# A graph network kernel: beside the last 56 edge rows, cosines are blended in PSUM and weighed from there, ScalarE weighs the gathered rows, and one PSUM bank takes the step sums

## The reference, cut to what matters

```python
def hetsann_conv(feat, src, dst, etype, edge_weight, W, Al, Ar, ...):
    h = typed_linear(feat[src], W, etype)
    ...
    agg = jax.ops.segment_sum(h3 * att * edge_weight, dst)     # cut
x = _layernorm(x + L0(x))          # two such layers, heads 8 and 1
# L1: cosine of the two ends of an edge weighs the sum over its neighbours
Wh = x @ W + b
sim = sum(Wh[row] * Wh[col]) / (|Wh[row]| * |Wh[col]|)
base = adj_v * softplus(deg_coeff[0] * deg_v + deg_coeff[1]) * (row != col)
prop_pos = segment_sum((base * relu(sim))[:, None] * Wh[col], row)
prop_neg = segment_sum((base * -relu(-sim))[:, None] * Wh[col], row)
x = _layernorm(x + scale * (c0 * prop_pos + c1 * prop_neg + c2 * Wh))
```

## Time and profile before

| | |
|---|---|
| median of 3 runs | 4801.52 us (4799.81 to 4803.82) |
| the profiled execution | 4794.28 us, its span 4792.6 us |
| the last 56 rows, first gather to last addition | 3336.5 to 4466.7 us |
| the other units, until the last product | to 4719.3 us |
| what follows: result turned back, last normalisation, store | to 4792.6 us |

### The profile page before, as it was taken

One profiled execution on the slowest core, in us unless ns is written; L12 is line 12 of the kernel. 1 busy time (PEld: TensorE's weight loads), 2 busy tenths in 40 slices (PEclk: granted clock), 3 DMA queues, 4 the chain that ended last, 5 costly groups with the idle time before them and its releaser, 6 DMA issues. The chain is left out here.

```text
span 4792.6 us, 63834 instructions
## 1 busy us (share of the span) xinstructions
PE 3187.0 (66%) x16141; PEld 1906.6 (40%) x16141; DVE 3208.5 (67%) x5876; ACT 1384.8 (29%) x2465; POOL 3339.1 (70%) x3216
## 2 busy tenths in 40 slices
PE   2667777777777777775555555554678767487795
PEld 2344445445545544543343444443323232222222
DVE  4676776767776677775555555554588777487686
ACT  2422232323232323233322122222233222132352
POOL 0277777777777777773577777775777777777573
PEclk6798888988888898887777777776688879688897
DMA  1233332323332333232222222223356545255583
GB/s 52 98 94 93 94 98 85 102 85 100 92 99 89 96 94 96 90 98 85 91 80 71 65 78 71 71 71 102 89 157 172 149 120 153 75 166 155 159 245 108
DMA packets 355069, 502.09 MB, mean 105 GB/s; under 512 B 92892, under 2 KB 214749, under 8 KB 354574
## 3 DMA queue, kind: packets, MB, share of 16 engines
q1 hardware_dynamic: 251453, 394.51, 25.4%
q0 software_dynamic: 100352, 102.96, 10.1%
q10 hardware_dynamic: 2896, 0.59, 0.1%
HBM read 290.63 MB, written 207.16 MB: 104 GB/s over the span
## 5 line engine op out<-in xcount | busy, mean ns | idle before, releaser
L809 POOL DMA_INDIRECT frows<-messages,fidx x2352 | 2277.5, 968 | 848.5 <-issue 669.3
L889 PE MATMUL fps_b<-hot_key,hot_lo 128*128 128x343 f32 x3136 | 1233.8, 502 | 407.1 <-PEq L70 403.3
L948 DVE TENSOR_TENSOR strip<-strip,fps_b 128x343 f32 x1568 | 787.0, 502 | 541.7 <-DVEq L70 516.5
L1091 POOL DMA_INDIRECT lrows<-messages,lidx x784 | 879.2, 1121 | 271.2 <-issue 223.7
L879 PE MATMUL fps_sum<-hot,frows 128*64 128x80 f32 x4704 | 551.1, 301 | 601.9 <-PEq L70 601.9
L824 ACT ACTIVATE turned<-fps_t 128x512 f32<-128x512 f32 (+1 forms) x754 | 431.6, 572 | 1741.2 <-ACTq L70 1738.8
L889 PEld LDWEIGHTS fps_b<-hot_key,hot_lo 128*128 128x128 f32 x3136 | 541.6, 206 | 728.8 <-issue 679.1
L879 PEld LDWEIGHTS fps_sum<-hot,frows 128*64 128x64 f32 x4704 | 521.9, 194 | 693.0 <-issue 693.0
L918 DVE TENSOR_SCALAR hot_key<-iota_f,edge 128x343 f32<-128x343 f32 x1574 | 750.9, 477 | 0.1
L1236 ACT ACTIVATE pos<-l_c,coeff 128x896 f32<-128x896 f32 x392 | 394.6, 1007 | 725.2 <-PE l_c L1140 725.2
L1140 PE MATMUL l_c<-unit_t,unit_g 64*128 64x448 f32 x1568 | 460.9, 667 | 148.5 <-DVE acc L1278 89.1
(11 more groups left out here) (186 smaller groups left out, 1741.7 us busy)
## 6 DMA issues: line engine op xcount, KB each, us to landing
adj<-turned SPq DMA_DIRECT2D x696, 256.0 KB
edge<-adj SPq DMA_DIRECT2D x294, 448.0 KB
adj_x<-adj SPq DMA_DIRECT2D x98, 448.0 KB
frows<-messages,fidx POOLq DMA_INDIRECT x2352, 2.4
messages<-msg SPq DMA_DIRECT2D x14, 1120.0 KB, 4.6
lrows<-messages,lidx POOLq DMA_INDIRECT x784
adj<-turned SPq DMA_DIRECT2D x58, 64.0 KB
wh_g<-wh_rows SPq DMA_DIRECT2D x56, 32.0 KB, 1.7
```

The lines of the kernel that those rows point to most:

```text
L809: pool.indirect_dma_start(rows[:, q, k, :], None, tab_l[l].ap(), bass.IndirectOffsetOnAxis(ap=idx[:, q, k:k + 1], axis=0)).then_inc(s_got[ ...
L889: pe.matmul(ps_b[n % KB][:, 0:NT * TWIN], hot_lo[:, s % 2, k, :], hot_key[:, n % KB, :], start=True, stop=True).then_inc(s_b, 1)
L948: dve.tensor_tensor(part, part, ps_b[n % KB][:, 0:NT * TWIN].rearrange("p (h w) -> p h w", w=TWIN), ALU.add).then_inc(v, 1)
L1091: pool.indirect_dma_start(rows[:, q, k, :], None, tab_l[1].ap(), bass.IndirectOffsetOnAxis(ap=idx[:, q, k:k + 1], axis=0)).then_inc(s_got[ ...
```

## The change

It touches `last_rows` alone. The order is planned with five units a row in place of six (`OWN`), and eight calls of `some` stand ahead of row 0. While rows run (units 0 to 255, `in_place`; before, 271 units were planned beside the rows), the blend is written back to the PSUM buffer of the cosines, and the weighing that follows it at once on VectorE reads that PSUM buffer, multiplies by `adj` and writes `con`. The cosines of unit u + 2, which need the PSUM buffer, then wait for the weighing of u, not for its blend. The comparisons of a row are one VectorE instruction that reads the node numbers from a PSUM bank (`l_iota`) and no longer multiplies by the weight. ScalarE multiplies the 14 gathered pieces by the weight in four parts, each behind the positive part of a unit; TensorE's sum waits for the last part (`s_wm`). The indices of row r + 4 are written when row r has landed. `l_iota` takes a bank, and the step sums have one bank, `l_o`, in place of two: the first product of each visit waits for the `kept` of the visit before.

```diff
-            OWN = 6
+            OWN = 5
+            PARTS = ((0, 4), (4, 8), (8, 11), (11, 14))
...
             plan.append(("hot", 0))
+            some(8, 0)
             for r in range(n_rows):
                 if r + 1 < n_rows:
                     plan.append(("hot", r + 1))
-                some(OWN - 1, r)
+                for j in range(len(PARTS)):
+                    some(1, r)
+                    plan.append(("wt", r, j))
                 plan.append(("sum", r))
-                some(1, r)
+                some(OWN - len(PARTS), r)
                 plan.append(("add", r))
...
-                ps_o = [psum(f"l_o{k}", [P, 512], s4) for k in range(2)]
+                ps_o = psum("l_o", [P, 512], s4)
+                ps_iota = psum("l_iota", [P, 512], s4)
...
+                def in_place(u):
+                    return u < alone
+
                 def weigh(eng, u):
                     eng.wait_ge(s_blend, u + 1)
                     eng.wait_ge(s_adj[u % NA], 16 * (u // NA + 1))
-                    eng.tensor_tensor(con[u % CB], con[u % CB], adj_b[u % NA], ALU.mult).then_inc(s_con[count[u][0]], 1)
+                    if in_place(u) and u >= CB:
+                        eng.wait_ge(s_prod, u - CB + 1)
+                    eng.tensor_tensor(con[u % CB], ps_c[u % 2][:, :, 0:SB] if in_place(u) else con[u % CB], adj_b[u % NA], ALU.mult).then_inc(s_con[count[u][0]], 1)
...
                         if u >= 2:
-                            pe.wait_ge(s_blend, u - 1)
+                            if in_place(u - 2):
+                                weighed(pe, u - 2)
+                            else:
+                                pe.wait_ge(s_blend, u - 1)
...
-                        if u == lo and k >= 2:
-                            pe.wait_ge(s_o_free, k - 1)
+                        if u == lo and k >= 1:
+                            pe.wait_ge(s_o_free, k)
...
-                        pe.wait_ge(s_got[r % RB], (r // RB + 1) * JT * 16).then_inc(s_idx_free[r % RB], 1)
+                        pe.wait_ge(s_wm, r + 1)
...
+                        elif event[0] == "wt":
+                            r, j = event[1:]
+                            if j == 0:
+                                act.wait_ge(s_got[r % RB], (r // RB + 1) * JT * 16)
+                                if r + RB < n_rows:
+                                    indices(r + RB)
+                            for k in range(*PARTS[j]):
+                                at = (first_row + r) * JT + k
+                                last = act.activation(rows[:, r % RB, k, :], rows[:, r % RB, k, :], ACT.Copy, scale=edge[:, A_W, at:at + 1])
+                            if j == len(PARTS) - 1:
+                                last.then_inc(s_wm, 1)
...
-                        if u >= CB:
+                        if not in_place(u):
                             dve.wait_ge(s_prod, u - CB + 1)
-                        dve.scalar_tensor_tensor(con[u % CB], ps_c[u % 2][:, :, 0:SB], coeff[:, 5:6], pos[:, u % 2, :, :], ALU.mult, ALU.add).then_inc(s_blend, 1)
+                        dve.scalar_tensor_tensor(ps_c[u % 2][:, :, 0:SB] if in_place(u) else con[u % CB], ps_c[u % 2][:, :, 0:SB], coeff[:, 5:6], pos[:, u % 2, :, :], ALU.mult, ALU.add).then_inc(s_blend, 1)
...
-                        for j in range(JT):
-                            at = (first_row + r) * JT + j
-                            last = dve.tensor_scalar(hot[:, r % 2, j, :], iota_f[:, 0:WIN], edge[:, A_REL, at:at + 1], edge[:, A_W, at:at + 1], ALU.is_equal, ALU.mult)
-                        last.then_inc(s_hot, 1)
+                        at = (first_row + r) * JT
+                        dve.tensor_tensor(hot[:, r % 2, :, :], ps_iota[:, 0:WIN].rearrange("p (o c) -> p o c", o=1).to_broadcast([P, JT, WIN]),
+                                          edge[:, A_REL, at:at + JT].rearrange("p (k o) -> p k o", o=1).to_broadcast([P, JT, WIN]), ALU.is_equal).then_inc(s_hot, 1)
...
                             if u < len(units):
                                 blend(u)
-                            if 1 <= u <= len(units) and count[u - 1][0] == 0:
+                                if in_place(u):
+                                    weigh(dve, u)
+                            if 1 <= u <= len(units) and not in_place(u - 1) and count[u - 1][0] == 0:
                                 weigh(dve, u - 1)
```

More of the change, by code:

```diff
@@ L1050, in last_rows @@
                 ps_c = [psum(f"l_c{k}", [P, 2, 512], s4) for k in range(2)]
-                ps_o = [psum(f"l_o{k}", [P, 512], s4) for k in range(2)]
+                ps_o = psum("l_o", [P, 512], s4)
+                ps_iota = psum("l_iota", [P, 512], s4)
                 def ls(name):
                     return sem(f"l_{name}")
-                s_idx, s_idx_free, s_rows_free = ([ls(f"{n}{q}") for q in range(RB)] for n in ("idx", "idx_free", "rows_free"))
+                s_idx, s_rows_free = ([ls(f"{n}{q}") for q in range(RB)] for n in ("idx", "rows_free"))
                 s_got = [sem(f"l_got{q}", True) for q in range(RB)]
-                s_hot, s_agg, s_add = (ls(n) for n in ("hot", "agg", "add"))
+                s_hot, s_wm, s_agg, s_add, s_iota = (ls(n) for n in ("hot", "wm", "agg", "add", "iota"))
                 s_c, s_pos, s_blend, s_prod, s_o_free = (ls(n) for n in ("c", "pos", "blend", "prod", "o_free"))
@@ L1149, in product @@
                                 pe.wait_ge(s_whg[c], 16 * len(groups_of(c)))
-                        if u == lo and k >= 2:
-                            pe.wait_ge(s_o_free, k - 1)
+                        if u == lo and k >= 1:
+                            pe.wait_ge(s_o_free, k)
                         weighed(pe, u)
                         for h in range(2):
-                            last = pe.matmul(ps_o[k % 2][h * F:(h + 1) * F, 0:SB], wh_g[:, 2 * p + h, :], con[u % CB][:, h, :],
+                            last = pe.matmul(ps_o[h * F:(h + 1) * F, 0:SB], wh_g[:, 2 * p + h, :], con[u % CB][:, h, :],
                                              start=(u == lo), stop=(u == hi), skip_group_check=True)
@@ L1285, in kept @@
                             dve.wait_ge(s_o_free, again[k][-1] + 1)
-                            dve.tensor_tensor(part, part, ps_o[k % 2][:, 0:SB], ALU.add).then_inc(s_o_free, 1)
+                            dve.tensor_tensor(part, part, ps_o[:, 0:SB], ALU.add).then_inc(s_o_free, 1)
                         else:
-                            dve.tensor_copy(part, ps_o[k % 2][:, 0:SB]).then_inc(s_o_free, 1)
+                            dve.tensor_copy(part, ps_o[:, 0:SB]).then_inc(s_o_free, 1)
                     def weights(r):
@@ L1344, in unit @@
                                           mom[:, 2, i].rearrange("p (c a b) -> p c a b", a=1, b=1).to_broadcast([P, CH, 2, F]), ALU.mult).then_inc(s_u, 1)
+                    dve.tensor_copy(ps_iota[:, 0:WIN], iota_f[:, 0:WIN]).then_inc(s_iota, 1)
+                    dve.wait_ge(s_iota, 1)
                     dve.memset(unit_t[:, :], 0.0).then_inc(s_zero, 1)
```

## The result

The changed kernel takes 4929.51 us (median of 4 runs, 4928.16 to 4934.43), the kernel before in the same session 4802.67 us: 1.0262 times as long, 95% interval 1.0244 to 1.028. That is 11 us above the 4918 us predicted.

A forecast was written before the change was run, and what follows sets the result against it. Beside the rows VectorE was taken to bind early, GpSimd's gathers later. Row 55 added 20 us later plus 99 us after the rows made +119 on 4794.3, 4913, which stands 7 below the median: 4918 us, range 4795 to 4990.

The forecast's parts named there:

- The gathers come free, and nobody takes them: GpSimd beside the rows: gathers could run at 17.4 us a row, but other engines need 19.7, so GpSimd waits.
- One bank: A visit's opening product waits for the last visit's kept, behind a blend and weighing; TensorE idles 4.4 us, its clock falls.
- A closing beside the rows: End of a visit while rows run: 4.3 us of VectorE waiting and 0.6 of work, 37 at 4.9 us.
- Behind the rows: From the last row's addition to the last product: 5 us a closing, 13 closings cost 65; stretch 99 us longer.
- closings without the clock: Rival, chance 0.25: TensorE stays at 2.4 GHz at the closings, 65 us less, 4853 us.
- The unit: VectorE beside the rows: blend 1.143, gap 0.15, weighing about 1.09, taken as 2.40 us a unit.
- The sum of a row: TensorE's sum waits for ScalarE's last weights; VectorE waits 2.4 us a row, before 1.64.
- The total: Whole kernel: +20 us at row 55's addition and +99 after it, +119 us, forecast 4918 us.
- Rows 5 to 55: Units, row work, sums, closings and pauses together 1004 us, 19.7 a row.
- The signs: Gathers near 0.95 us, GpSimd idle, some 50 sums_t waits of 3 to 5 us, clock below 0.87, short visits 2.9 us a unit.
- the gathers decide: Rival, chance 0.14: other engines keep within 17.4 us a row, 4780 us; 4707 if closings cost nothing besides.
- no difference: Rival, chance 0.05: closings and sums cost a third less, row 55 added 76 us earlier, 4801 us.

The follow-up runs named there:

- run 8: The changed kernel with two banks for the step sums, comparison from SBUF, and blend in SBUF with weighing one event later: 4872.6 us, 1.0137 of the kernel before.
- run 2: The changed kernel with two banks for the step sums again, the row's comparison reading node numbers from SBUF: 4746.8 us, 0.988 of the kernel before.
- run 4: The changed kernel, one bank kept, but blend writes SBUF and weighing reads two SBUF buffers one event later: 4953.3 us, 1.0308 of the kernel before.
- run 1: The changed kernel with kept moved ahead of the blend of unit hi + 4 on VectorE, still one bank: 4756.2 us, 0.9898 of the kernel before.
- run 3: The kernel before with one bank for the step sums and nothing else changed: 4957.4 us, 1.0319 of the kernel before.
- run 6: The kernel of run 2, but ScalarE weighs in three parts and the row's sum stands a unit later: 4739.0 us, 0.9858 of the kernel before.
- run 9: The kernel of run 1, but ScalarE weighs in three parts and the row's sum stands a unit later: 4744.3 us, 0.9877 of the kernel before.
- run 7: The kernel of run 2 with six units a row, three ScalarE parts and the sum a unit later: 4738.6 us, 0.9864 of the kernel before.
- run 10: The kernel of run 2, but the row's 14 comparisons multiply by the weight on VectorE, ScalarE weighs nothing: 4760.1 us, 0.9911 of the kernel before.

## Why the prediction was right, by its steps

**The gathers come free, and nobody takes them.** Right: 0.949 us each, GpSimd waiting for buffers. What weighing from PSUM gives with two banks is the difference of runs 8 and 2, 128 us of row stretch, near the 139 us of the earlier trace rows. The change, with its one bank, keeps only the difference of run 4 and itself: 28 us. The rule of the Trainium skill ("SBUF — State Buffer", Who interferes with whom) on VectorE instructions with two SBUF inputs agrees with runs 8 and 2 too, with gathers of 1164 and 987 ns; that rule alone would have forecast a faster kernel.

**One bank.** This step decided the sign, and runs 1, 2 and 3 show it from three sides: move kept by one place and 173 us go, give the bank back and 183 go, take the bank from the kernel before and 152 come. The mechanism was as written, the order on VectorE: TensorE was to stand idle for 4.4 us, and the 35 waits for `sums_t` beside the rows are 4.42 us on average. The size of the cost was somewhat off. A closing beside the rows costs 5.3 to 5.6 us, where 4.9 stood in the sum: 4.70 of waiting and 0.61 of work in the one shown, and by the rows, of which those with one closing come every 20.8 us (median) and those without every 15.2. Behind the rows it costs (290.5 - 217.9)/13 = 5.6 against 5.0, and run 2, with two banks, takes 216.3 us for the same 115 units. The clock is the greater part of this miss. I took 1.2 GHz in three cases of four; it was more. In the closing shown above the 4.70 us are the 3.1 of the step and what the clock adds in the same rows: the product takes 1.76 in place of 0.97 us, and ScalarE starts 1.92 in place of 1.07 us after the cosines, together 1.64. Of the 40 closings beside the rows 37 have a product of over 1.3 us (36 of them the full 1.76) and 31 have cosines of over 1.4 us behind it; of the 13 from unit 276 on it is 11 and 13. The rival "closings without the clock" falls with that; no run took the clock away alone, so its share is read, not tested.

**The unit.** 2.40 us were too many. In the closing shown above weighings start 1.18 and 1.19 us after their blend, where 1.143 + 0.15 was taken. The gap between blend and weighing was 0.03 us in all 256 units, not the 0.15 of the earlier trace rows. The code of the earlier trace rows also takes the semaphore back, with a decrement; whether that is the reason no run shows. A blend that writes PSUM takes 1.154 us against 1.143. A weighing that reads it takes 1.091, near the 1.089 of the earlier trace rows, although that row is a comparison and not the multiply for which the prediction takes it. The Trainium skill ("VectorE: DVE Perf Modes", The TRN2 errata) gives a PSUM source 62 cycles more, by my estimate 0.065 us; measured it is 0.014 above the 1.077 of the SBUF multiply. Undisturbed, a unit takes 2.20 us.

**The sum of a row.** 2.7 us of waiting for 2.4 (in 24 of the 56 rows; the others are mixed with closings and pauses). ScalarE's instruction of 128x64 takes 336 ns, above both bounds of the earlier trace rows, but a part of four takes 1.05 us as assumed, because they overlap. Runs 6 and 9 take ScalarE's part of the wait away and gain 7 and 14 us of row stretch.

**The total.** Rows 5 to 55: 987 us for 1004. The shorter unit takes 235 times 0.20, 47 us; the dearer closings give back 15 to 26, the dearer sums 15. Rows 0 to 4: 21 us later where 5 were charged; the finishing of the first pieces hid less of the closings than I had assumed, for in run 2, without waits for a bank, row 4 is added 145 us after the first gather, against 162. So 16 us too little stand against 17 too much, and that the stretch grew by 19 us where 20 were predicted is luck. Behind the rows, unit 276 began 34 us later relative to the last addition (26 and the two closings, 8, were predicted), and the 13 closings make up the rest. Both stretches together grew by 127 us for 119. The other 8 us by which the profiled execution is longer lie ahead of the change. The last line of the sum has a slip: 4913 and 7 are 4920, not 4918.

**The signs.** Gathers at 0.95 us, 50 recorded waits for `sums_t` of 3.0 to 5.7 us, GpSimd waiting for buffers and short visits of 2.9 to 3.0 us a unit are as foretold. The clock is a poor sign: from 3600 to 3800 us it was 0.85 for the 0.87 of the earlier trace rows, but over the whole row stretch it rose.

The rivals "the gathers decide" and "no difference" were the same kernel with closings that cost less beside the rows; runs 1 and 2 come near that case and gave 4756 and 4747 us, where 4707 stood for closings that cost nothing. Even then the units' chain, not the gathers, held many rows: in both runs undisturbed rows come every 15.2 us, where 14 gathers take 17.4 or more.

The best kernels of the study are 6 and 7, at 0.986 of the kernel before: the change with its second bank back.

## What to carry to other kernels

When a buffer is given up, look for the instruction that frees the one left, and for what stands ahead of it in its queue: here 0.6 us of work held TensorE for 3 to 6 us because it stood behind a blend and a weighing that themselves depended on TensorE. If the buffer must go, move the freeing instruction ahead first, which adds no instruction and here decided between 1.026 and 0.990. And a relieved engine is worth only what its consumers can take: weighing from PSUM was worth 128 us of row stretch with two banks, and 28 with one.

## What the hardware showed that I had not expected

VectorE's gap between a blend and the weighing that waits for it was 0.03 us, where two dependent instructions of another part stood 0.15 apart. After waits of 3.0 to 5.7 us TensorE ran 42 of the 53 opening products wholly at 1.2 GHz (1.76 us at a granted 0.50), 9 partly (1.22 to 1.70 us) and 2 not at all (0.97 us). With one comparison of 1.3 us a row that reads two SBUF operands the gathers' mean is 0.987 us (run 2), with one that reads PSUM 0.950 (run 1), which is 29 us over 784; with the 14 short comparisons of run 10 it is 0.957.
